# Two attentions on one core: both halves of a projected tile in front of the value product, and their copy in front of the first sum

## What is computed

```python
qkv = (x @ qkv_w.T).reshape(b, t, 3, H, HD)
q, k, v = ...
raw = jnp.einsum('bhid,bhjd->bhij', q, k)
scores = sips_alpha[0] * jnp.tanh(raw / sips_beta[0])
soft_bits = jnp.tanh(x @ hex_w.T)
scores = scores + lam * (jnp.einsum('bid,bjd->bij', soft_bits, soft_bits) / 2.0)[:, None]
hexc = jnp.tanh(x @ q6_w.T)
lat = jnp.einsum('bid,hde,bje->bhij', hexc, Mh, hexc) / 6.0
scores = scores + lat * (jax.nn.sigmoid(scale_logit) * 2.0)
scores = jnp.where(causal, scores, -jnp.inf)
out = jnp.einsum('bhij,bhjd->bhid', softmax(scores), v)
```

## Time and profile before

| | |
|---|---|
| time, median of 3 runs | 3957.81 us (3957.8 to 3959.95) |
| profiled execution | 3962.9 us, span 3960.8 us |
| busy, share of the span | PE 93%, ACT 88%, DVE 63%, PEld 37%, POOL 16% |
| tanh (979), 544 times | 1995 ns each |
| exp (990), 544 times | 1937 ns each |
| sum (1059), 2176 times | 740 ns each |
| first attention | from about 117 us to 2178 us |
| tensor clock over the span | 0.98 of full speed |

### The profile page before, as it was taken

One profiled execution on the slowest core, in us unless ns is written; L12 is line 12 of the kernel. 1 busy time (PEld: TensorE's weight loads), 2 busy tenths in 40 slices (PEclk: granted clock), 3 DMA queues, 4 the chain that ended last, 5 costly groups with the idle time before them and its releaser, 6 DMA issues. The chain is left out here.

```text
span 3960.8 us, 62584 instructions
## 1 busy us (share of the span) xinstructions
PE 3672.6 (93%) x22185; PEld 1463.5 (37%) x22200; DVE 2505.6 (63%) x4392; ACT 3494.6 (88%) x2970; POOL 622.9 (16%) x658
## 2 busy tenths in 40 slices
PE   6799999999999999999998799879999999999898
PEld 2233333333333333323222566522222222222576
DVE  5688888888888888888877476623232323232576
ACT  2799999999999999999999466579999999999566
POOL 3112211221112111200000255500000000000233
PEclk9899999999999999999999899989999999999999
DMA  5322322222322232121111477632222222222331
GB/s 166 108 81 63 90 78 85 63 82 78 93 70 67 85 90 70 57 80 48 56 40 34 149 187 196 152 88 86 61 82 65 77 70 73 74 73 65 105 96 54
DMA packets 274758, 340.52 MB, mean 86 GB/s; under 512 B 40148, under 2 KB 207927, under 8 KB 274173
## 3 DMA queue, kind: packets, MB, share of 16 engines
q1 hardware_dynamic: 274432, 336.38, 29.3%
HBM read 207.97 MB, written 128.25 MB: 85 GB/s over the span
## 5 line engine op out<-in xcount | busy, mean ns | idle before, releaser
L1059 DVE SCALAR_TENSOR_TENSOR att_prob<-att_tanh,alpha,ps 128x512 f32<-128x512 f32 x2176 | 1515.1, 740 | 387.7 <-ACT att_tanh L979 191.2
L979 ACT ACTIVATE att_tanh<-ps,rbeta 128x2048 f32<-128x2048 f32 x544 | 1085.0, 1995 | 66.3 <-PE ps L904 62.3
L985 ACT ACTIVATE att_prob<-ps 128x1024 f32<-128x1024 f32 x1088 | 1054.4, 1021 | 21.3 <-PE ps L904 5.1
L990 ACT ACTIVATE att_prob<-att_prob 128x2048 f32<-128x2048 f32 x544 | 1053.7, 1937 | 11.0 <-DVE att_prob L1059 10.4
L937 PE MATMUL ps<-att_prob,att_v 128*32 128x512 f32 (+3 forms) x8064 | 911.4, 535 | 1.9 <-ACT att_prob L990 1.9
L904 PE MATMUL ps<-att_q,att_k 99*128 99x512 bf16 (+5 forms) x2816 | 624.0, 342 | 12.6 <-ACT att_tanh L979 7.9
L1042 DVE TENSOR_TENSOR att_prob<-att_prob,keep 128x512 f32<-128x512 f32 (+1 forms) x320 | 187.5, 586 | 576.1 <-ACT att_prob L985 575.0
L914 PE MATMUL ps<-att_f,att_g 75*128 75x512 bf16 (+3 forms) x1408 | 423.4, 346 | 43.1 <-DVE att_prob L1059 36.2
L904 PEld LDWEIGHTS ps<-att_q,att_k 96*128 96x128 bf16 (+1 forms) x2816 | 229.4, 97 | 442.8 <-ACT att_prob L985 230.6
L904 PE MATMUL ps<-q,att_k 99*128 99x512 bf16 (+5 forms) x1216 | 292.5, 357 | 6.4 <-ACT att_tanh L979 3.8
L914 PEld LDWEIGHTS ps<-att_f,att_g 75*128 75x128 bf16 x1408 | 125.0, 97 | 440.5 <-DVE att_prob L1059 416.1
(11 more groups left out here) (187 smaller groups left out, 3736.1 us busy)
## 6 DMA issues: line engine op xcount, KB each, us to landing
att_v<-v_ones SPq DMA_DIRECT2D x106, 256.0 KB
att_k<-k_parts SPq DMA_DIRECT2D x106, 192.0 KB
o_t<-att_on SPq DMA_DIRECT2D x512, 32.0 KB, 1.8
v_ones<-mid_vs SPq DMA_DIRECT2D x64, 256.0 KB, 3.3
att_q<-q_parts SPq DMA_DIRECT2D x84, 192.0 KB
att_k<-k_parts SPq DMA_DIRECT2D x106, 128.0 KB
v_ones<-att_vs SPq DMA_DIRECT2D x96, 128.0 KB, 2.7
q_parts<-mid_parts SPq DMA_DIRECT2D x128, 96.0 KB, 1.9
```

Source lines behind the costliest of these rows:

```text
L979: th.done(act.activation(tanh_s[:, S % 2], ps[:, QK0:QK0 + HQ], ACT.Tanh, scale=kn["rbeta"][:, 0:1]))
L985: pr.done(act.activation(prob[:, S % R, 2 * pair:2 * pair + 2], ps[:, bank:bank + 2], ACT.Exp, scale=float(HD) ** -0.5))
L990: pr.done(act.activation(prob[:, (S - 1) % R], prob[:, (S - 1) % R], ACT.Exp))
L1059: sc.done(dve.scalar_tensor_tensor(prob[:, S % R, h], tanh_s[:, S % 2, h], kn["alpha"][:, 0:1], ps[:, E0 + h % 2], ALU.mult, ALU.add))
```

## The change

In PE's loop place a moves from behind the second extra product to the front of the step, ahead of the value product. As place b of the step before ends that step, the two halves of a unit such as "12b 13a" then follow each other on PE. In DVE's `sums` the copy moves from between head 1 and head 2 to the front of head 0. `normalise` stays where it was. Nothing else differs: the same instructions are issued, with the same waits on the same semaphores.

```diff
@@ PE's loop over the steps
             for S in range(N + LAG):
                 if layer == 1 and S + 1 < N:
                     scores(S + 1, 0)
+                if layer == 0 and S < N:
+                    piece(S, "a")
                 if S >= LAG:
                     weigh(S - LAG)
                 if layer == 0 and S < N:
                     extra(S, 0)
                     extra(S, 1)
-                    piece(S, "a")
                     if S + 1 < N:
                         scores(S + 1, 0)
                 if S + 1 < N:
@@ DVE's sums(S, due)
                 copied = unit_at(S)
                 if copied is not None and unit(copied)[1] == "g":
                     copied = None
+                if copied is not None:
+                    evict(copied)
                 for h in range(HQ):
-                    if h == 2:
-                        if copied is not None:
-                            evict(copied)
-                        else:
-
-                            normalise(due, 1)
+                    if h == 2 and copied is None:
+
+                        normalise(due, 1)
                     th.wait(dve, S)
                     ex.wait(dve, S * HQ + h)
```

## The result

The changed kernel takes 3977.65 us (median of 5 runs, 3975.39 to 3980.85) against 3957.81 us (5 runs, 3957.72 to 3959.95). The ratio is 1.0048, with a 95% interval of 1.0037 to 1.0058: it is slower, by some 19 us. The profiled execution took 3980.85 us, with a span of 3978.8, that is 18.0 more than the span before.

What follows compares the result with a forecast made beforehand. A loop through PE and VectorE was taken to bound steps with pieces; per set 0.67 − 0.47 − 0.40 + 1.55 + 0.15 = 1.50 us, over twelve sets +18, 3957.8 to 3976 us (range 3956 to 3994).

Steps and rivals of the forecast that it cites:

- ring L: Loop through PE and VectorE from one extra product of head 0 to the next: 4.17 us against 3.94.
- steps 9 to 12: Step 9: the feature tile's 512-column half ahead of the value product delays exp, +0.15 us a set (0 to 0.9).
- steps 13 to 16: First run of steps with pieces: stalls of 1.44 us instead of about 0.77, +0.67 a set.
- steps 17 and 18: Step 17: normalising product no longer meets POOL's splitting, 0.42 instead of 1.15; −0.47 us a set (−0.47 to +0.26).
- steps 19 to 21: Step 20: half a no longer stands in front of the scores, −0.40 us a set (−0.44 to 0).
- steps 25 to 33: Second run, steps 26 to 32: stalls of 3.70 us instead of 2.15, +1.55 a set.
- rivals A: Faster: sums run earlier, the loop holds half a at 3.73 us; decides under 4.02; kernel 3923 us; chance 0.10.
- C: No difference: a quarter of half a's 0.44 hides in b's 0.53, loop 4.02 to 4.05, about 3960 us; chance 0.12.
- Two of the signs: In full-loop steps, head 3's extra product load waits about 0.4 us longer; the tanh waits about 0.5 for scores.
- rival D: Copy blocks the sums if half a or POOL's buffer is late: up to 0.42 a step, 4026 us; chance 0.03.
- rival B: Half a's weight loads on PE stand open: one, 0.15 in each of 120 loops, 3994 us; both 4012; chance 0.09.
- the lag at step 13: Time from step 13's tanh to its extra product of head 0: 2.03 us forecast, 1.59 before.

Runs made afterwards that it cites:

- E3: Kernel before, plan shifted: both halves of a unit in one step, half a behind the second extra product, copy before the next step's first sum; 3912.53 us.
- E1: Changed kernel with the copy left between head 1 and head 2, so only half a is moved; 4023.51 us, ratio 1.0158 to before.
- E2: Kernel before with only the copy moved in front of the first sum, half a left behind the second extra product; 4113.6 us, ratio 1.0387.
- E8: Kernel before with half a moved between the value product and the extra product of head 0, copy left in place; 4063.3 us, one run.
- E7: Kernel before with POOL's splitting of the tile ending in step 16 cut to 16 of 512 columns in eleven sets; 3954.43 us, ratio 0.9987.
- E5: Kernel before with the whole change applied only in steps 24 to 33 of a set; 3979.95 us, ratio 1.0046.
- E4: Kernel of E3 with half a moved behind the next step's scores, before the extra product of head 2; 3912.89 us, ratio 0.9879 to before.
- E6: Kernel of E3 with the feature tile's halves at 8b and 9b and half a behind the scores in steps 24 to 31; 3911.83 us, ratio 0.9877.

## Why the prediction was right, point by point

The forecast was 3976 and 18 us more; measured 3977.65, and 18.0 us in the spans. The sign, the cause and the sum stand. The terms, a set each:

```
                      forecast   found
ring L                 4.17      4.14
steps 9 to 12         +0.15     -0.05
steps 13 to 16        +0.67     +0.44
steps 17 and 18       -0.47     -0.34
steps 19 to 21        -0.40     -0.01
steps 25 to 33        +1.55     +1.28
steps 1 and 2          0        +0.09
sum                   +1.50     +1.41
```

- **The ring.** Its links were right to 0.02, and a takes 0.43. The first sum starts 0.50 after ex0, not 0.53. That goes with the copy in front of it: it is 0.50 in the changed kernel, where half a is elsewhere, and in E3, where it stands behind ex1; it is 0.53 in the kernel before and in E1, where the copy stands between the sums. With L at 4.14 rivals A (under 4.02) and C (4.02 to 4.05) fall. E1 (4.38), E2 (4.68) and E3 (3.71) give the three other lengths that the same links add up to: 4.35, 4.71 and 3.71. E8 (4.47 for 4.38) shows that a costs 0.1 more where its load starts only with its product. Two of the signs were off in size: ex3's load waits 0.20 longer for the second sum (0.56 for 0.36), not 0.4, and the tanh waits 0.38 for the scores, not 0.5.
- **The copy is free in front of the first sum.** Right: nothing waits for it, and it ends 0.9 before that sum; rival D falls. Without the early a the cover is gone, and that costs 0.94 a step (E2: 1.47 instead of 0.53). The prediction had put it at up to 0.42, the copy's own length; it left out that the copy also waits for a's product (0.69 after its start).
- **The rule on weight loads.** The Trainium skill, "TensorE: Matmul & The Clock Gate", Part 3 ("The mechanism"), has the line that lets a weight load overlap only a product in another row group (its first paragraph names the background weight buffer as a second way). In the changed kernel the loads of b and a start at 840.38 with ex3 still to run, take 0.85 for four, and b and a together take 0.43 + 0.53 to the value product. The loads of these full 128-row tiles ran ahead: b's product starts 0.23 behind its load. The measurement decides, and rival B (4.32 and more) falls.
- **Steps 13 to 16.** Found 0.23 less. Step 12 already lasted 3.84 instead of 3.68, which took that much from the lag at step 13 (1.89 for the 2.03 forecast), so step 14 stalled less. That part is the same time, paid two steps earlier; 0.06 is the ring at 4.14.
- **Step 9.** The forecast had the exp later and forgot what the same move gives: the scores of step 10 no longer stand behind the 512-column half. The rows of set 5, and below them those of steps 19 and 20:

```profile
815.63 1.41 DVE L1059 SCALAR_TENSOR_TENSOR att_prob<-att_tanh,alpha,ps 128x512 f32<-128x512 f32 x2 [1.19 <-PE ps L914]
816.61 1.99 ACT L980 ACTIVATE att_tanh<-ps,rbeta 128x2048 f32<-128x2048 f32 x1
818.98 1.91 ACT L991 ACTIVATE att_prob<-att_prob 128x2048 f32<-128x2048 f32 x1
...
851.93 1.95 ACT L980 ACTIVATE att_tanh<-ps,rbeta 128x2048 f32<-128x2048 f32 x1
853.01 0.16 PEld L937 LDWEIGHTS ps<-att_prob,att_v 128*32 128x32 f32 x8 [0.36 <-issue]
854.00 0.12 PEld L914 LDWEIGHTS ps<-att_f,att_g 75*128 75x128 bf16 x2 [0.84 <-DVE att_prob L1059]
```

Step 9 lasts 3.66 (812.95 to 816.61) instead of 3.92, and the exp starts at 818.98, 6.03 after the tanh of step 9, where it was 6.27. But ex0 is later against its tanh from there on, and step 12 pays 0.16. Together about nothing.
- **Step 17.** Right in its parts:

```profile
845.42 1.16 POOL L1095 TENSOR_TENSOR att_parts<-att_rem,att_parts 128x512 bf16<-128x512 f32 x1 [0.18 <-POOL att_parts L1093]
848.35 0.42 DVE L1030 TENSOR_TENSOR att_oq<-att_ot,att_rc 128x256 f32<-128x256 f32 x1
850.11 1.91 ACT L991 ACTIVATE att_prob<-att_prob 128x2048 f32<-128x2048 f32 x1
...
L1030 DVE TENSOR_TENSOR att_oq<-att_ot,att_rc 128x256 f32<-128x256 f32 x128 | 54.0, 422 | 2.2
```

POOL ends at 846.58, 1.8 before the product, which takes 0.42; its mean over the span falls from 490 to 422 ns, twelve times 0.73 over 128. From ex0 (846.43) to exp (850.11) are 3.68, as forecast. The lag was 2.36, not 2.23, since b(16) is a product of the f unit, whose load started 0.32 behind ex3's, and the value product another 0.60 later. E7 shows the same cause alone. The rule of the Trainium skill ("SBUF — State Buffer", "SBUF: two separate sides"), that a GpSimd operation and a VectorE one with two SBUF inputs hold a shared port in turn, agrees with both.
- **Step 20 was mis-sized**, the largest miss: −0.40 forecast, the steps 19 to 21 together gave −0.01. The forecast took 0.44 off for the earlier scores and allowed 0.04 for what step 19 passes on. The scores did come earlier against ex0, by 0.71 (the tanh 1.75 after it instead of 2.46), but ex0 of step 20 came 0.61 later against its tanh (2.65 for 2.04), so step 20 lasts 4.40 instead of 4.50, and step 19 lasts 0.09 more. The lag was there at step 19: 854.00 − 851.93 = 2.07, where it was 1.19. The tanh of step 19 came 0.35 earlier because exp 17 no longer waited, but PE's own chain over step 18, with half a in it, had not become shorter: the value product starts 1.08 behind the tanh (853.01), where it was 0.19. What ACT gains at one step is lag at the next. E7 shows the effect by itself: 0.18 of 0.73 given back.
- **Steps 1 and 2** were not in the sum. The longer run leaves more lag at its end (2.63 instead of 2.01 at step 32), and 0.09 of it is still paid in step 1 of the next set.
- **Cancelling.** The two runs cost 0.50 less than forecast, steps 17 to 21 gave 0.52 less, step 9 cost 0.20 less, and step 1 cost 0.09 more. The sum is better than its parts, and owes that to chance in part.

## What to carry to other kernels

Before work is moved on a full engine, close the ring: follow one step from an instruction to its successor in the next step, and see which instructions are links of it and which run beside it. Half a lay under two sums of another engine and cost nothing; in front of the value product the same instruction cost its full 0.43 us, in about 120 steps. A wait of 0.24 was taken out by putting 0.43 in; shifting both halves into one step, so that the copy fell into VectorE's idle time and half a stayed under the sums, removed the wait for nothing and gave 1.2%.

## What the runs showed that was not expected

**The clock fell in step 20.** In E2 (12 sets), E8 (9), E5 (3) and E7 (1) TensorE's granted clock went from 1.00 to 0.50 (from 2.4 to 1.2 GHz) within step 20, and the step took 7.7 to 9.0 us in E2, 5.9 to 7.5 in E8, 7.1 to 7.2 in E5 and 5.9 in E7; without a fall it takes 4.4 to 4.7 in the last three. In one fall of E5 step 20 took 7.19 and step 21 5.15, together 4.2 us more than in its other sets. In E5 the code of these steps, and in E7 all of PE's code, is that of the kernel before, whose profiled execution has no such fall, and in E5's window 852 to 854, ahead of the fall, PE was busy for 1.87 of 2.00 us. Ahead of it stand steps 17 and 18, and then step 20 itself, with small masked products and waits for sums. What decides between the sets was not tried. It is a cost beside the ring, and the profile's clock column has to be read before a sum is blamed: in E7 one such set made the mean of step 20 look like 4.52 instead of 4.38.

**Stalls move.** E4 and E6 each removed a stall that the timeline shows plainly (0.3 us at step 16, 0.28 at step 9) and gained nothing. With ACT's own pace making 124.20 of the 126 us of a set, a lag that is allowed to build up in one place is paid at the next place with less room.
